# Turning probabilities and attention results by DMA crossbar transposes in place of TensorE, in an attention layer with residual and layer norm

## The chip, the cores and the metric

The kernel runs on one core of one Trainium2 chip. The metric is the device time of one execution in microseconds. The times given for a kernel are those of several runs; one further execution was recorded by the hardware profiler.

## What is computed

64 graphs of 128 nodes, each node with 512 features in 16 heads of 32. Masked attention, output projection, residual, layer norm:

```python
q = heads(x @ Wq + bq); k = heads(x @ Wk + bk); v = heads(x @ Wv + bv)
scores = jnp.einsum('bhqd,bhkd->bhqk', q, k) * scale
scores = jnp.where(mask[:, None] == 0, -jnp.inf, scores)
attn = jax.nn.softmax(scores, axis=-1)
out = jnp.einsum('bhqk,bhkd->bhqd', attn, v)
out = out.transpose(0, 2, 1, 3).reshape(b, s, D_MODEL)
x = _layernorm(x + out @ Wo + bo, axis=-1)
```

All arrays are float32.

## The kernel before

Float32 products are made from pairs of float16: a value is split into a high part (rounded to float16, by ScalarE, ACT) and a low part (the remainder, by VectorE, DVE), and TensorE (PE) multiplies hi x hi, hi x lo and lo x hi into one float32 sum.

The work runs in 32 groups of 2 batches. A group has 8 steps; step s takes the scores of 4 heads of one batch (s // 4 is the batch, s % 4 the heads). Every engine runs an order written out by hand, with semaphores between the engines; groups 2 to 29 are a loop whose body is two groups. In the same step as the attention of group g, PE also works on a projection bank: `TASKS` says which. The Q and K banks (24 matmuls of 256 columns) and V banks (12 of 512) are those of group g+1; the Y banks are the output projection of a batch finished earlier.

The path of the four heads of a step, before:

1. PE: `scores`, four matmuls of a stacked Q by a stacked K (`q_stack`, `k_stack`, where high and low parts lie under one another on the partitions) into `score_ps`.
2. DVE: `masked_max`, mask added and row minimum taken, four instructions each with an accumulator read.
3. ACT: `exponentials`, four activations into `probs`, float32.
4. PE: `transpose_probs`, four float32 transposes into `pT_ps`.
5. ACT: `high_part_probs` makes `pT_hi` from PSUM. DVE: `low_part_probs` makes `pT_lo` from PSUM.
6. PE: `attend`, eight small matmuls into `av_ps`. The attention of step s-1 is done in step s, behind the scores of step s+1.
7. DVE: `head_norm`. GpSimd (POOL): `attn_sum`, into `attn`.

When a batch's four steps are through, PE turns `attn` by four float32 transposes into `aT_ps` (`transpose_attn`); ACT and DVE split it into `aT_hi` and `aT_lo`; the Y bank multiplies by the output weights; DVE adds the residual and takes the moments (`y_and_moments`); POOL normalizes and SP stores. POOL also makes the residual (`x_res`) and the low part of the next inputs (`xT_lo`).

The Q and K stacks of group g+1 are made by DMA in SyncE's (SP's) queue. `spread_rows` takes eight DMAs of 64 KB for each of Q and K, from the split parts in `part` to the stack; `copy_rows` waits until they have landed and then doubles rows in the stack (two DMAs of 256 KB for Q, one of 512 KB for K). The scores of step 0 wait for both. SP's other DMAs load x in two layouts and the adjacency, and store the result.

## Time and profile before

| | |
|---|---|
| runs | 1017.27 us median of 3 (1017.2 to 1017.75) |
| the profiled execution's own time | 1017.49 us |
| its span in the trace | 1015.5 us |
| granted TensorE clock | 0.987 of full speed |
| busy: PE, DVE, ACT, POOL | 94%, 83%, 66%, 36% |
| instructions of PE's matmul row | 8968 |

A busy share is the part of the span in which an engine has an instruction under way. Matmuls are pipelined, so the distance between the starts of two of them says more than their durations. The trace gives for idle time of an engine what ended it, as "<-engine tile". "issue" means that no other engine's event did. SPq is SyncE's queue; its rows are the times for which issuing a DMA held the queue, and the landing of a DMA is told apart from that.

### The profile page before, as it was taken

The numbers are of one execution on the slowest core, as the hardware profiler recorded it, in microseconds if no ns is written. First come the engines' busy times: TensorE is split into PE (matmuls) and PEld (weight loads), VectorE is DVE, ScalarE is ACT, GpSimd is POOL, SyncE is SP. The second block draws the span as 40 slices with busy tenths as digits, with TensorE's granted clock in tenths as the row PEclk, the third lists the DMA queues.
The fourth block names the chain that finished last, engine by engine and source line by source line (L and its number), as shares of the span: only waits on it lengthen the run. The fifth ranks groups of instructions, "written<-read, shape, count | busy, mean of one in ns | idle before, by whom it ended". The sixth has DMA issues, their size and how long they took to land.

```text
span 1015.5 us, 29711 instructions
## 1 busy us (share of the span) xinstructions
PE 958.5 (94%) x8968; PEld 716.7 (71%) x8968; DVE 840.9 (83%) x3449; ACT 675.2 (66%) x1745; POOL 370.4 (36%) x643
## 2 busy tenths in 40 slices
PE   6799999999999999999999999999999999999974
PEld 4566776767777776777767777776777777677752
DVE  5478987888988888988888888788898888898885
ACT  5456776767767666776767767676776766677662
POOL 0043343334334333334333434333433433333332
PEclk9899999999999999999999999999999999999988
DMA  6535344454444445344445434445444444534420
GB/s 244 151 109 129 108 131 121 134 136 129 114 123 126 129 132 150 94 129 124 133 124 150 118 106 139 120 134 137 129 114 123 123 131 133 151 93 129 116 58 32
DMA packets 103790, 127.02 MB, mean 125 GB/s; under 512 B 12561, under 2 KB 82193, under 8 KB 99217
## 3 DMA queue, kind: packets, MB, share of 16 engines
q1 hardware_dynamic: 103696, 126.15, 44.1%
q14 instruction: 80, 0.65, 0.2%
q8 instruction: 14, 0.23, 0.1%
HBM read 42.21 MB, written 16.78 MB: 58 GB/s over the span
## 4 chain that ended last, share of the span: by engine, by line
PE 64%; issue 14%; DVE 12%; POOL 5%; DMA 1%; SPq 1%; POOLq 1%; DVEq 0%; ACT 0%; ACTq 0%
PE proj_ps L732 45%; PE pT_ps L830 8%; PE score_ps L732 4%; PE av_ps L732 4%; DVE masked L599 3%; PE aT_ps L744 2%; DVE pT_lo L585 2%; POOL x_res L373 2%; POOL attn L382 1%; DVE stats L630 1%; DVE kT_lo L576 1%; SPq L295 1%; POOL y L403 1%; DVE y L626 1%; DVE attn_parts L613 1%
## 5 line engine op out<-in xcount | busy, mean ns | idle before, releaser
L491 ACT ACTIVATE probs<-masked,minus_max 128x128 f32<-128x128 f32 x1024 | 325.6, 391 | 66.6 <-DVE minus_max L599 65.0
L382 POOL TENSOR_TENSOR attn<-attn_parts 128x128 f32<-128x128 f32 x256 | 116.9, 457 | 610.1 <-DVE attn_parts L613 610.1
L599 DVE CUSTOM_DVE_ANT_0 masked<-score_ps,mask 128x128 f32<-128x128 f32 x1024 | 236.0, 286 | 119.2 <-PE score_ps L732 73.6
L501 ACT ACTIVATE pT_hi<-pT_ps 128x512 f16<-128x512 f32 x256 | 152.7, 596 | 171.6 <-PE pT_ps L830 166.3
L585 DVE SCALAR_TENSOR_TENSOR pT_lo<-pT_ps,pT_hi 128x512 f16<-128x512 f32 x256 | 174.2, 681 | 0.4 <-ACT pT_hi L501 0.4
L830 PE MATMUL pT_ps<-ident,probs 128*128 128x128 f32 x1024 | 163.8, 283 | 2.6 <-ACT probs L491 0.9
L732 PE MATMUL proj_ps<-xT_hi,wq_hi 128*128 128x256 f16 x512 | 141.4, 276 | 7.9 <-DVE wq_lo L701 7.9
L732 PE MATMUL proj_ps<-xT_lo,wq_hi 128*128 128x256 f16 x512 | 141.5, 276 | 0.0
L732 PE MATMUL proj_ps<-xT_hi,wq_lo 128*128 128x256 f16 x512 | 141.5, 276 | 0.0
L732 PE MATMUL proj_ps<-xT_hi,wk_hi 128*128 128x256 f16 x512 | 139.5, 273 | 0.0
L732 PE MATMUL proj_ps<-xT_hi,wk_lo 128*128 128x256 f16 x512 | 139.5, 273 | 0.0
L732 PE MATMUL proj_ps<-xT_lo,wk_hi 128*128 128x256 f16 x512 | 139.5, 273 | 0.0
L613 DVE TENSOR_TENSOR attn_parts<-av_ps,inv_sum 128x256 f32<-128x256 f32 x256 | 108.7, 425 | 11.3
L732 PE MATMUL av_ps<-v_parts,pT_hi 128*128 128x65 f16 x1024 | 93.4, 192 | 19.5 <-DVE pT_lo L585 19.5
L732 PE MATMUL score_ps<-k_stack,q_stack 128*128 128x128 f16 x1024 | 99.7, 220 | 12.5 <-DMA k_stack<-k_stack 9.0
L830 PEld LDWEIGHTS pT_ps<-ident,probs 128*128 128x128 f32 x1024 | 108.2, 141 | 4.2 <-issue 3.0
L732 PEld LDWEIGHTS score_ps<-k_stack,q_stack 128*128 128x128 f16 x1024 | 77.6, 98 | 40.4 <-issue 18.8
L732 PE MATMUL proj_ps<-wo_hi,aT_hi 128*128 128x512 f16 x256 | 98.4, 385 | 1.4 <-DVE aT_lo L559 1.4
L732 PE MATMUL proj_ps<-wo_hi,aT_lo 128*128 128x512 f16 x256 | 98.3, 384 | 0.0
L732 PE MATMUL proj_ps<-wo_lo,aT_hi 128*128 128x512 f16 x256 | 98.2, 384 | 0.0
L732 PE MATMUL proj_ps<-wv_hi,xT_hi 128*128 128x512 f16 x256 | 97.0, 379 | 0.0
L732 PE MATMUL proj_ps<-wv_lo,xT_hi 128*128 128x512 f16 x256 | 97.0, 379 | 0.0
(62 smaller groups left out, 1832.2 us busy)
## 6 DMA issues: line engine op xcount, KB each, us to landing
xT_raw<-x_cols SPq DMA_DIRECT2D x32, 512.0 KB, 4.8
q_stack<-q_stack SPq DMA_DIRECT2D x64, 256.0 KB, 3.5
k_stack<-k_stack SPq DMA_DIRECT2D x32, 512.0 KB, 4.4
x_in<-x_rows SPq DMA_DIRECT2D x32, 512.0 KB, 3.9
out<-y SPq DMA_DIRECT2D x64, 256.0 KB, 2.2
q_stack<-qT_hi SPq DMA_DIRECT2D x128, 64.0 KB, 2.0
q_stack<-qT_lo SPq DMA_DIRECT2D x128, 64.0 KB, 2.0
k_stack<-kT_hi SPq DMA_DIRECT2D x128, 64.0 KB, 2.2
```

The lines of the kernel that those rows point to most:

```text
L295: sp.dma_start(heads[QUAD * quad:QUAD * (quad + 1), :, j, :], part[n, h][rows]).then_inc(spread[n][par], 16)
L373: pool.tensor_tensor(x_res[:, par, b], x_in[par][:, b], b_out[:], ALU.add).then_inc(res_made, 1)
L382: pool.tensor_tensor(attn[b][:, c * P:(c + 1) * P].rearrange("p (h d) -> p h d", h=HC), attn_parts[s % 2][:, :, V_LO:V_LO + DH], attn_part ...
L403: pool.tensor_scalar(y[b][:], y[b][:], minus_mean[b][:], inv_std[b][:], ALU.add, ALU.mult).then_inc(ln_done, 1)
L491: ins = act.activation(probs[s % 2][:, j], masked[s % 2][:, j], ACT.Exp, bias=minus_max[s % 2][:, j:j + 1], scale=-1.0)
L501: act.activation(pT_hi[s % 2][:], pT_ps[s % 2][:], ACT.Copy, scale=P_UP).then_inc(pT_hi_done, 1)
L585: dve.scalar_tensor_tensor(out=pT_lo[s % 2][:], in0=pT_ps[s % 2][:], scalar=P_UP, in1=pT_hi[s % 2][:], op0=ALU.mult, op1=ALU.subtract).the ...
L599: ins = dve.tensor_tensor_reduce(masked[s % 2][:, j], score_ps[s % 2][:, j], mask[par][:, s // KC], -EXP_SCALE, 3.0e38, ALU.add, ALU.min, ...
L613: dve.tensor_tensor(attn_parts[s % 2][:], av_view[:, :, 0:2 * DH], inv_sum[s % 2][:].unsqueeze(2).to_broadcast([P, HC, 2 * DH]), ALU.mult) ...
L732: return pe.matmul(dst, lhsT, rhs, start=first, stop=last)
L744: ins = pe.transpose(aT_ps[:, c], attn[b][:, c * P:(c + 1) * P], ident[:])
L830: ins = pe.transpose(pT_ps[s % 2][:, j], probs[s % 2][:, j], ident[:])
```

## The change

Probabilities are no longer turned by PE. ACT splits the high part of `probs` in row layout into the left half of a float16 tile `p_pair`, DVE puts the low part into the right half, and SP issues one DMA crossbar transpose (`dma_start_transpose`) of the 128 x 1024 tile into `pT`, from which PE's `attend` reads. `p_pair` has 2 buffers, `pT` has 4. The attention result goes the same way through `a_pair` and `aT`, one transpose a batch. Step s on PE is now: bank, scores of step s+1, attention of step s-2. The PSUM freed by the transposes gives four projection banks in place of two and two for the attention product. `TASKS` puts the Y banks in slots 4 and 7. The mask instruction becomes a scalar_tensor_tensor with a broadcast tile as second input. Loads, stores and copies have new places in SP's order.

```diff
-    TASKS = {0: (Q, 0), 1: (Q, 1), 2: (K, 0), 3: (K, 1), 4: (Y, 1), 5: (V, 0), 6: (V, 1), 7: (Y, 0), 8: (Y, 1)}
+    TASKS = ((Q, 0), (Q, 1), (K, 0), (K, 1), (Y, 0), (V, 0), (V, 1), (Y, 1))
+    NB = 4
...
-        probs = [sb(f"probs{i}", [P, HC, S], F32) for i in range(2)]
-        pT_hi = [sb(f"pT_hi{i}", [P, HC, S], F16) for i in range(2)]
-        pT_lo = [sb(f"pT_lo{i}", [P, HC, S], F16) for i in range(2)]
+        probs = [sb(f"probs{i}", [P, HW], F32) for i in range(2)]
+        p_pair = [sb(f"p_pair{i}", [P, 2 * HW], F16) for i in range(2)]
+        pT = [sb(f"pT{i}", [P, 2 * HC, S], F16) for i in range(NT)]
...
+            def turn_probs(g, s):
+                u = unit(g, s)
+                sp.wait_ge(p_lo_done, u + 1)
+                sp.sem_inc(sync_goes, 1)
+                wait(sp, av_done, u - NT + 1)
+                sp.sem_inc(sync_goes, 1)
+                sp.dma_start_transpose(pT[s % NT][:], p_pair[s % 2][:]).then_inc(p_turned[s % NT], 16)
+            def turn_attn(g, b):
+                n = batch(g, b)
+                sp.wait_ge(a_lo_done, n + 1)
...
+                sp.dma_start_transpose(aT[b][:], a_pair[b][:]).then_inc(a_turned[b], 16)
...
+                for s in range(SLOTS):
+                    before, slot = back(g, s, 1)
+                    if exists(before):
+                        turn_probs(before, slot)
...
+                    if s == 2 and at_least(g, 1):
+                        turn_attn(g - 1, 0)
...
+                    if s == 3 and has_next(g):
+                        spread_rows(Q, g + 1, nxt)
+                    if s == 4 and has_next(g):
+                        copy_rows(Q, g + 1, nxt, k + par)
+                    if s == 5 and at_least(g, 1):
+                        turn_attn(g - 1, 1)
+                    if s == 5 and has_next(g):
+                        spread_rows(K, g + 1, nxt)
+                    if s == 6 and has_next(g):
+                        copy_rows(K, g + 1, nxt, k + par)
...
+            def high_part_probs(g, s):
+                act.wait_ge(exp_done, unit(g, s) + 1)
+                before, slot = back(g, s, 2)
+                if exists(before):
+                    act.wait_ge(p_turned[slot % NT], 16 * turn_round(before, slot))
+                act.activation(p_pair[s % 2][:, 0:HW], probs[s % 2][:], ACT.Copy, scale=P_UP).then_inc(p_hi_done, 1)
...
             def low_part_probs(g, s):
-                dve.wait_ge(pT_hi_done, unit(g, s) + 1)
-                dve.scalar_tensor_tensor(out=pT_lo[s % 2][:], in0=pT_ps[s % 2][:], scalar=P_UP, in1=pT_hi[s % 2][:],
-                                         op0=ALU.mult, op1=ALU.subtract).then_inc(pT_out, 1)
+                dve.wait_ge(p_hi_done, unit(g, s) + 1)
+                dve.scalar_tensor_tensor(out=p_pair[s % 2][:, HW:2 * HW], in0=probs[s % 2][:], scalar=P_UP,
+                                         in1=p_pair[s % 2][:, 0:HW], op0=ALU.mult,
+                                         op1=ALU.subtract).then_inc(p_lo_done, 1)
...
-                dve.tensor_scalar(mask[par][:], adj_in[par][:], 0.0, MASKED, ALU.is_equal,
-                                  ALU.mult).then_inc(mask_made, 1)
+                dve.scalar_tensor_tensor(out=mask[par][:].rearrange("p b t -> p (b t)"),
+                                         in0=adj_in[par][:].rearrange("p b t -> p (b t)"), scalar=0.0,
+                                         in1=masked_out[:].to_broadcast([P, TOK]), op0=ALU.is_equal,
+                                         op1=ALU.mult).then_inc(mask_made, 1)
...
-            def transpose_probs(g, s):
-                u = unit(g, s)
-                pe.wait_ge(exp_done, u + 1)
-                wait(pe, pT_out, u - 1)
-                for j in range(HC):
-                    ins = pe.transpose(pT_ps[s % 2][:, j], probs[s % 2][:, j], ident[:])
-                ins.then_inc(pT_done, 1)
...
             def group(g, par, k):
                 nxt = 1 - par
                 for s in range(SLOTS):
...
+                    step_bank(g, s, par)
                     if s < SLOTS - 1:
                         scores(g, s + 1, par, k)
-                    else:
+                    elif has_next(g):
                         scores(g + 1, 0, nxt, k + par)
...
+                    before, slot = back(g, s, 2)
+                    if exists(before):
+                        attend(before, slot, par if s >= 2 else nxt)
```

DVE's order in a group, before and after (in `group` of the vector block; `bank_to_split` and `filled` are the slot whose bank is split there):

```python
# before
masked_max(g, s, par)
low_part_bank(g, filled, par)
head_norm(g, s - 2)
low_part_probs(g, s - 1)
# after
low_part_probs(before, slot)      # before, slot = back(g, s, 1)
masked_max(g, s, par)
low_part_bank(g + 1, *TASKS[s - 1], nxt)
head_norm(before, slot)           # before, slot = back(g, s, 3)
```

DVE's instructions in the first group of the loop, in steps 1 and 2. Each masked head is a pair of rows (the instruction and its accumulator read). Before:

```order
L599 ISA masked1,minus_max1<-score_ps1,mask0 128x128
L599 ISA minus_max1 128x1
L608 RECIPROCAL inv_sum1<-av_ps 128x4
L118 REGISTER_ALU
L613 TENSOR_TENSOR attn_parts1<-av_ps,inv_sum1 128x256
L566 ISA
L576 SCALAR_TENSOR_TENSOR qT_lo<-proj_ps1,b_qk_up,qT_hi 128x256 x2
L585 SCALAR_TENSOR_TENSOR pT_lo0<-pT_ps0,pT_hi0 128x512
L591 REGISTER_ALU
L599 ISA masked0,minus_max0<-score_ps0,mask0 128x128
L599 ISA minus_max0 128x1
```

After, from the split of the Q bank in step 1 to the first masked head of step 2:

```order
L526 SCALAR_TENSOR_TENSOR qT_lo<-proj_ps0,b_qk_up,qT_hi 128x256 x2
L553 REGISTER_ALU
L554 RECIPROCAL inv_sum0<-av_ps0 128x4
L84 REGISTER_ALU
L558 TENSOR_TENSOR attn_parts0<-av_ps0,inv_sum0 128x256
L511 ISA
L512 SCALAR_TENSOR_TENSOR a_pair0<-attn0,a_pair0 128x512
L533 SCALAR_TENSOR_TENSOR p_pair1<-probs1,p_pair1 128x512
L539 REGISTER_ALU
L546 ISA masked0,minus_max0<-score_ps0,mask0 128x128
L546 ISA minus_max0 128x1
```

Before, the low part at the end of step 1 is that of step 0 (buffer 0), ahead of the masked scores of step 2 (buffer 0). After, the low part ahead of the masked scores of step 2 is that of step 1 (buffer 1), the step whose scores were masked last.

SP's issues in the same group, from the Q copies on. ISA and REGISTER_ALU rows are waits and their registers. Before:

```order
L306 DMA q_stack1<-q_stack1 32x4096
L307 DMA q_stack1<-q_stack1 32x4096
L289 REGISTER_ALU
L295 DMA k_stack1<-kT_hi 32x4x256
L295 DMA k_stack1<-kT_lo 32x4x256
```

After, from the end of the Q spreads to the start of the K spreads:

```order
L256 DMA q_stack1<-qT_lo 32x1024
L270 REGISTER_ALU
L275 DMA_TRANSPOSE pT3<-p_pair1 128x8x128
L261 ISA
L265 DMA q_stack1<-q_stack1 32x4096
L266 DMA q_stack1<-q_stack1 32x4096
L270 REGISTER_ALU
L275 DMA_TRANSPOSE pT0<-p_pair0 128x8x128
L279 REGISTER_ALU
L284 DMA_TRANSPOSE aT1<-a_pair1 128x8x128
L252 REGISTER_ALU
L256 DMA k_stack1<-kT_hi 32x1024
```

One transpose now stands between the Q spreads and the Q copies, and two between the Q copies and the K spreads.

## Rows read from the trace of the kernel before

**Rows 1.** The page: its first line, and the busy line.

```profile
span 1015.5 us, 29711 instructions
PE 958.5 (94%) x8968; PEld 716.7 (71%) x8968; DVE 840.9 (83%) x3449; ACT 675.2 (66%) x1745; POOL 370.4 (36%) x643
```

**Rows 2.** Table by stages, 100 to 900 us: busy of each engine (instructions), clock, DMA share, GB/s.

```profile
100.00:900.00 800.00, 781.72 (x7443) 590.95 (x7442) 685.63 (x2836) 550.89 (x1432) 308.58 (x530) 1.00 0.45 127
```

**Rows 3.** Timeline of DVE: the mask in group 15 and in group 30.

```profile
510.51 1.28 DVE L646 TENSOR_SCALAR mask<-adj_in 128x256 f32<-128x256 int32 x1
...
961.86 0.28 DVE L646 TENSOR_SCALAR mask<-adj_in 128x256 f32<-128x256 int32 x1
```

**Rows 4.** Waits of DVE: us in total, times, longest.

```profile
DVE masked L599 <- issue: 37.8, 14, 4.2
```

**Rows 5.** Timeline of PE: scores, transposes, next bank, next scores (start, us).

```profile
503.57 0.39 PE L732 MATMUL score_ps<-k_stack,q_stack 128*128 128x128 f16 x4
...
504.02 0.63 PE L830 MATMUL pT_ps<-ident,probs 128*128 128x128 f32 x4
504.49 0.27 PE L732 MATMUL proj_ps<-xT_hi,wk_hi 128*128 128x256 f16 x1
...
507.11 0.39 PE L732 MATMUL score_ps<-k_stack,q_stack 128*128 128x128 f16 x4
```

**Rows 6.** Timeline of DVE, a step with y and its moments.

```profile
511.71 0.28 DVE L599 CUSTOM_DVE_ANT_0 masked<-score_ps,mask 128x128 f32<-128x128 f32 x1
...
512.55 0.08 DVE L599 DVE_READ_ACCUMULATOR2_ANT minus_max<- 128x1 f32 x1
...
513.10 0.68 DVE L585 SCALAR_TENSOR_TENSOR pT_lo<-pT_ps,pT_hi 128x512 f16<-128x512 f32 x1
513.70 0.68 DVE L626 SCALAR_TENSOR_TENSOR y<-proj_ps,x_res 128x512 f32<-128x512 f32 x1
...
515.59 0.29 DVE L599 CUSTOM_DVE_ANT_0 masked<-score_ps,mask 128x128 f32<-128x128 f32 x1
```

**Rows 7.** Timeline of ACT, one row; groups by line, two rows (busy, mean ns).

```profile
512.67 1.28 ACT L491 ACTIVATE probs<-masked,minus_max 128x128 f32<-128x128 f32 x4 [0.33 <-DVE minus_max L599]
...
L701 DVE SCALAR_TENSOR_TENSOR wo_lo<-w_land,wo_hi 128x512 f16<-128x512 f32 x4 | 2.5, 684 | 0.0
...
L534 ACT ACTIVATE wo_hi<-w_land 128x512 f16<-128x512 f32 x4 | 2.2, 618 | 0.0
```

**Rows 8.** Timeline of SP's queue: Q copy, last two K spreads, K copy, store.

```profile
508.96 0.56 SPq L306 DMA_DIRECT2D q_stack<-q_stack  x1
...
514.42 0.60 SPq L295 DMA_DIRECT2D k_stack<-kT_hi  x1
515.06 0.60 SPq L295 DMA_DIRECT2D k_stack<-kT_lo  x1
517.08 0.51 SPq L304 DMA_DIRECT2D k_stack<-k_stack  x1
520.51 0.36 SPq L312 DMA_DIRECT2D out<-y  x1
```

**Rows 9.** DMA issues: times, KB each, median us to landing.

```profile
q_stack<-q_stack SPq DMA_DIRECT2D x64, 256.0 KB, 3.5
k_stack<-k_stack SPq DMA_DIRECT2D x32, 512.0 KB, 4.4
```

**Rows 10.** Timeline of POOL in group 15.

```profile
506.53 0.46 POOL L382 TENSOR_TENSOR attn<-attn_parts 128x128 f32<-128x128 f32 x1 [1.96 <-DVE attn_parts L613]
506.95 1.27 POOL L373 TENSOR_TENSOR x_res<-x_in,b_out 128x512 f32<-128x512 f32 x1
...
510.49 1.16 POOL L259 TENSOR_TENSOR xT_lo<-xT_raw,xT_hi 128x512 f16<-128x512 f32 x1
```

**Rows 11.** The masked scores' line: duration min/median/max, first and last start.

```profile
L599 DVE CUSTOM_DVE_ANT_0 masked<-score_ps,mask x1024: 275/286/293, 37.2 to 994.5; 128x128 f32<-128x128 f32 x171
```

**Rows 12.** DMA from 503.5 to 508 us: packets, MB, share of 16 engines.

```profile
q1 hardware_dynamic: 1008, 0.46, 39.6%
```

More of the change, by code:

```diff
@@ L118, in wait, with at_least @@
             eng.wait_ge(sem, value)
+    def at_least(g, n):
+        return not isinstance(g, int) or g >= n
     def has_next(g):
@@ L124, in has_x_next2, with back, exists, all_groups @@
         return not isinstance(g, int) or g < LAST - 1
-    def all_groups(eng, group, first=None, last=None):
-        (first or group)(0, 0, 0)
+    def back(g, s, lag):
+        return (g, s - lag) if s >= lag else (g - 1, s - lag + SLOTS)
+    def exists(g):
+        return not isinstance(g, int) or g >= 0
+    def all_groups(eng, group):
+        group(0, 0, 0)
         group(1, 1, 0)
@@ L134, in all_groups @@
         group(NG - 2, 0, NG // 2 - 1)
-        (last or group)(NG - 1, 1, NG // 2 - 1)
+        group(NG - 1, 1, NG // 2 - 1)
     with ExitStack() as ctx:
@@ L211, in build_program @@
         stored = [sem(f"stored{i}") for i in range(2)]
+        p_turned = [sem(f"p_turned{i}") for i in range(NT)]
+        a_turned = [sem(f"a_turned{i}") for i in range(2)]
         const_made = sem("const_made")
@@ L358, in _ @@
             all_groups(sp, group)
-            store(LAST, 0)
-            store(LAST, 1)
+            turn_probs(LAST, SLOTS - 1)
+            turn_attn(LAST, 0)
+            store(LAST - 1, 1)
+            turn_attn(LAST, 1)
+            for b in range(GB):
+                store(LAST, b)
             for b in range(GB):
@@ L429, in _ @@
-            pool.memset(ident[:], 0.0).then_inc(const_made, 1)
-            pool.wait_ge(const_made, 1)
-            pool.affine_select(out=ident[:], in_=ident[:], compare_op=ALU.not_equal, fill=1.0, base=0,
-                               pattern=[[-1, P]], channel_multiplier=1).then_inc(const_made, 1)
+                    before, slot = back(g, s, 3)
+                    if exists(before):
+                        attn_sum(before, slot)
+                    if s == 1 and at_least(g, 2):
+                        normalize(g - 2, 1)
@@ L632, in y_and_moments @@
                 dve.wait_ge(stats_done, n + 1)
[L633 removed]
+                if at_least(g, 1):
                     dve.wait_ge(ln_done, batch(g - 1, b) + 1)
@@ new lines, in group @@
+                    before, slot = back(g, s, 1)
+                    if exists(before):
+                        low_part_probs(before, slot)
+                    masked_max(g, s, par)
+                    if s > 0 and TASKS[s - 1][0] != Y and has_next(g):
+                        low_part_bank(g + 1, *TASKS[s - 1], nxt)
+                    before, slot = back(g, s, 3)
+                    if exists(before):
+                        head_norm(before, slot)
+                    if s == 0 and at_least(g, 2):
+                        y_and_moments(g - 2, 1, par)
@@ L685, in group @@
+                    if s == 1 and at_least(g, 1):
+                        low_part_attn(g - 1, 0)
+                    if s == 4 and at_least(g, 1):
+                        low_part_attn(g - 1, 1)
+                    if s == 5 and at_least(g, 1):
+                        y_and_moments(g - 1, 0, nxt)
+                    if s == 1 and not at_least(g, 1):
                         dve.wait_ge(b_out_mm, 1)
@@ new lines, in y_bank @@
+            def y_bank(g, b):
+                pe.wait_ge(a_turned[b], 16 * (g + 1))
+                dst = proj_ps[bank_of(Y, b)]
+                for ki in range(KC):
+                    if not at_least(g, 1):
+                        weight_made("o", ki)
+                    mm(dst[:], aT[b][:, ki], w_hi["o"][:, ki], ki == 0, False)
+                    mm(dst[:], aT[b][:, ki], w_lo["o"][:, ki], False, False)
+                    ins = mm(dst[:], aT[b][:, KC + ki], w_hi["o"][:, ki], False, ki == KC - 1)
+                ins.then_inc(y_mm, 1)
@@ new lines, in _ @@
+            pe.wait_ge(w_loaded["o"][0], 16)
+            pe.wait_ge(bias_made, 2)
+            for ki in range(KC):
+                ins = mm(b_out_ps[:], b_v_wide[:, ki], w_raw["o"][:, ki], ki == 0, ki == KC - 1)
+            ins.then_inc(b_out_mm, 1)
+            scores(0, 0, 0, 0)
+            all_groups(pe, group)
+            attend(LAST, SLOTS - 2, LAST % 2)
+            pe.wait_ge(y_summed, batch(LAST - 1, 0) + 1)
+            y_bank(LAST, 0)
+            attend(LAST, SLOTS - 1, LAST % 2)
```

529 lines of the change are left out of this document (206 added, 323 removed).

## The prediction

> **What bounds the kernel now.** I read the page first: TensorE (PE) is busy 94% of the span, VectorE (DVE) 83% [rows 1]. The table over 100 to 900 us says that this is no average over unlike stages: PE 782 of 800 us, at full clock, DVE 686, DMA engines 45% [rows 2]. The mask is made once a group; two of them stand 451.4 us and 15 groups apart [rows 3], so a group (2 batches, 8 steps) takes 30.1 us, against 31 of them in the span. In the list of waits DVE stands idle 14 times 2.7 us, once per turn of the loop, under "issue" [rows 4]. TensorE's instruction stream is the bound; every other engine fits around it.
>
> **What the change takes from TensorE.** The four probability transposes of a step hold PE from 504.02 to 504.49, 0.47 us [rows 5]. Ten such sets a group (8 for probabilities, 2 for the attention result) are 4.7 us, and PE needs 25.4 us a group. If PE stayed the bound, 32 groups would save 150 us: 867 us. So the question is what the next bound is.
>
> **The loop between DVE and ScalarE (ACT).** Before, the high and low parts of the probabilities were split after the transpose, and DVE wrote them last in its step. Now both split in row layout, and DVE's order has the low part of step s-1 *ahead* of the masked scores of step s. With that, one closed loop runs through both engines: low part(s-1), masked(s), exp(s), high part(s), low part(s). Its pieces: low part 0.60 from start to next start, masked 0.92 from the first head's start to the end of the fourth head's accumulator read [rows 6], hand-over 0.04, exp 1.28 [rows 7], then the high part. That reads SBUF now instead of PSUM; the same form on the same engine is wo_hi<-w_land, 0.62 us, and DVE's low part from SBUF is wo_lo<-w_land, 0.68 [rows 7], what it took from PSUM, so the new source saves nothing. With two more hand-overs: 0.60 + 0.92 + 0.04 + 1.28 + 0.05 + 0.62 + 0.05 = 3.56 us a step. PE's step would be 3.07 (3.54 from scores to scores, less 0.47). Two steps of a group carry y_and_moments, which the gap in the loop doesn't hold: from the last masked head to the low part 0.55, y and its moments 1.89, low part 0.60, masked 0.84 [rows 6], 3.9 in all, 0.3 too much. Loop alone: 8 x 3.56 + 0.6 = 29.1 us a group. Of 30.1 this gives back 1.0 us, not 4.7.
>
> **The DMA queue of SyncE (SP).** SP issues in program order, and each issue holds it: a spread DMA 0.60 (0.64 from one to the next), eight of them 5.2, copies 0.5 to 0.6, a store 0.36 [rows 8]. A group costs SP 16 x 0.64 + 3.7 = 13.9 us now, plus waits for landings. Ten transposes come on top, woven between spreads and copies. Call t what one transpose holds the queue for. No transpose by DMA stands in the trace. Lower bound 0.36 (the shortest issue); upper bound 2.9, eight blocks of 128x128 at that price each; I take 0.64, the spread's, the nearest row that moves rows between SBUF partitions with a broken pattern. Landing: at least 3.5 us, the 256 KB copy's [rows 9].
>
> Which wait ends last in a group? The scores of the next group need the K stack. I follow SP from the masked scores of step 3, which start 3 x 3.56 + 0.3 = 11.0 us into the group. The low part of step 2 is just done (0.1); its transpose t; eight Q spreads 5.2; the Q copies wait for the last spread to land, 1.4 beyond its issue (515.06 to 517.08 for K [rows 8], less 0.6), in which the next transpose fits; two copies 1.2; then the step 4 transpose and one of the attention result, 2t; eight K spreads 5.2; landing 1.4, again with a transpose under it; the K copy lands after 4.4 [rows 9]; scores 0.4 [rows 5]. Sum 19.3 + 3t. The period is therefore 11.0 + 19.3 + 3t = 30.3 + 3t, 32.2 us with t = 0.64. The loop needs 29.1 and waits 3 us per group for the K stack. That wait also covers DVE's loop-turn gap of 2.7 us, which costs nothing more; without that cover it would be 1.35 a group. Before, SP reached the K spreads right behind the Q copies, and PE's slower step gave them time.
>
> **DVE against GpSimd (POOL).** The mask took 0.28 us when POOL was idle and 1.28 beside POOL's 1.16 us xT_lo, ending 0.14 after it [rows 3, 10]: DVE was kept out. The low part of the probabilities, which read PSUM and one SBUF tile, now reads two SBUF tiles; the mask no longer has its old form. If it meets the same exclusion, then in step 2 POOL's sum (0.46) and x_res (1.27) start 2.4 us after the masked scores and end at 4.1, where the low part could start at 2.96: 1.1 us later. Steps 4, 6 and 7 have a residual or xT_lo too (3.2 us more), but there the K stack is waited for anyway. Bounds: 0, or 1.1 plus 0.5 for the meeting in step 1. I take 1.1: 33.3 us a group.
> The Trainium skill, "SBUF — State Buffer", section "Who interferes with whom", speaks for the collision: a DVE instruction with two SBUF inputs contends with a GpSimd instruction that reads SBUF, and with at most one, outside the fast modes, it doesn't. By this rule 33.3 stands, and without it the sum is 32.2 a group, 1090 us. The trace shows the lock only on the mask.
>
> **The sum.** First masked scores at 37.2 us [rows 11] as before; first group 32.0 (no y terms, no collision); 30 groups x 33.3 = 999; seven steps of the last group 25.5 (there PE had no projections, and before ran steps of 2 to 3.6 us; the loop doesn't get shorter); from the last masked scores to the end 21 us before [rows 1, 11], and two more round trips of a DMA transpose at 3.5 each in place of PE transposes, less what PE took, about 27. That is 1121 span, and with the 2.0 us between span and execution (1017.49 against 1015.5; the median of the runs is 1017.27) 1123 us. What a measurement can't tell from no change is 0.2%, 2 us.
>
> **Rivals.**
> *The queue is held longer (t near 1.6).* For: a transpose has 128 rows x 8 blocks, 1024 pieces, a spread 128. Against: the copy of 8 KB rows and the spread of 512 B rows hold SP alike, so pieces don't seem to be priced. Period 30.3 + 4.8 + 1.1 = 36.2, time about 1210. From t = 2 on SP itself is the bound (13.9 + 10t + 2.8 us), and t = 2.9 would give 46 us a group, about 1510.
 No row here shows it.
> *The DMA engines.* In 503.5 to 508 the spreads moved 0.46 MB in 1008 packets at 39.6% of 16 engines [rows 12], 1.78 us in all: 1.0 us for 256 KB by bytes, 1.8 for 1024 packets. Ten of them and today's 13.5 (45% of 30.1) make 24 to 32 of 33.3 us: full, not over. Beyond 2.0 us a transpose they bind; landings later than 5.7 us after the low part (3.56 - 0.1 + 0.92 + 0.04 + 1.28 + 0.05) already hold the high part two steps on, since p_pair has two buffers. At 2.5 us: 38.5 a group, about 1285; mild lateness 1160.
> *Faster.* The K stack arrives within the loop, and the loop alone rules: 37 + 31 + 30 x 29.1 + 52 + 2 = 995 us. It decides once the period is under 29.7. For: PE has 4.7 us to spare, and its projections can run ahead through four banks. Against: even t = 0 leaves 30.3, so spreads or landings would have to be shorter than their rows.
> *TensorE stays the bound* (867): only if the loop didn't exist; the order on DVE excludes it.
>
> **Chances.** Forecast as built, 1080 to 1160: 0.50. Longer hold: 0.20. DMA engines or late landings, 1160 to 1290: 0.15. Faster: 0.08. Within 0.2%: 0.03. The rest (0.04) is below 1080 but slower, or far above. The range 1055 to 1250 leaves out faster, same, and the worst of both upper cases, 0.19. Faster 0.08, same 0.03, slower 0.89.
>
> **What will show it.** PE well under 85% busy; masked scores 3.6 us apart inside a group and about 3 us extra ahead of a group's first, with PE's scores waiting for k_stack's DMA; DVE's low part waiting for ACT's high part in most steps; low parts longer than 0.68 where x_res or xT_lo runs; SP's issues near 24 us a group. Wrong if: transpose issues take much more than 0.64 (then the K stack is later by three times that), the low part shows waits for the DMA's release of p_pair (DMA engines), or steps repeat in under 3.4 us.

## The result and the profile after

The changed kernel takes 1322.22 us (median of 4 runs, 1314.91 to 1323.66), the kernel before 1017.39 in the same comparison (4 runs): ratio 1.298, interval 1.293 to 1.303. I had forecast 1123 us and a range that ended at 1250. The direction was right, the size was not: 305 us are lost, and I had seen 106 of them coming.

The page of the changed kernel, against [rows 1]:

```profile
span 1321.6 us, 28124 instructions
PE 925.9 (70%) x7688; PEld 620.5 (47%) x7688; DVE 860.4 (65%) x3449; ACT 693.3 (52%) x1745; POOL 431.9 (33%) x642
...
q1 hardware_dynamic: 392464, 210.07, 72.9%
...
SPq 38%; issue 14%; PE 14%; DMA 14%; DVE 12%; ACT 7%; DVEq 1%; POOL 0%; ACTq 0%; POOLq 0%
SPq L256 22%; DMA k_stack<-k_stack 11%; PE proj_ps L657 11%; SPq L275 11%; DVE masked L546 5%; ACT probs L460 5%; SPq L284 3%; ACT p_pair L470 3%; PE score_ps L657 2%; DVE kT_lo L526 2%; SPq L266 1%; SPq L265 1%; DVE p_pair L533 1%; DVE qT_lo L526 1%; DVE a_pair L512 1%
```

No engine is full any more. The last two rows are the chain that ended last: 38% of the span lies in SyncE's queue, most of it on the spreads (L256), then on the transposes (L275, L284), and 11% on the landing of the K copy.

The same table and stretch as [rows 2]:

```profile
100.00:900.00 800.00, 576.62 (x4834) 387.65 (x4832) 532.73 (x2164) 430.94 (x1092) 280.31 (x408) 0.87 0.75 162
```

The mask, once a group as in [rows 3], from 200 to 900 us (duration min/median/max in ns, first and last start):

```profile
L584 DVE SCALAR_TENSOR_TENSOR mask<-adj_in,masked_out x18: 414/415/416, 228.0 to 897.1; 128x256 f32<-128x256 int32 x18
```

A group takes (897.1 - 228.0) / 17 = 39.4 us where it took 30.15: 9.2 us more, in 31 groups 285 of the 305 us. All comparisons below go by this period.

The waits (us in all, times, longest):

```profile
DVE p_pair L533 <- ACT p_pair L470: 268.4, 165, 5.0
...
PE score_ps L657 <- DMA k_stack<-k_stack: 202.0, 29, 7.2
ACT p_pair L470 <- DMA pT<-p_pair: 177.9, 92, 4.5
```

TensorE waits 7 us for the K stack in nearly every group.

SyncE's queue in group 12 (counted from 0), from the transpose of step 2 on. Masked scores of the group start at 513.13, those of step 3 at 525.42:

```profile
525.72 1.24 SPq L275 DMA_TRANSPOSE pT<-p_pair  x1
527.10 0.56 SPq L256 DMA_DIRECT2D q_stack<-qT_hi  x1
...
531.50 0.59 SPq L256 DMA_DIRECT2D q_stack<-qT_lo  x1
532.36 1.26 SPq L275 DMA_TRANSPOSE pT<-p_pair  x1
533.79 0.52 SPq L265 DMA_DIRECT2D q_stack<-q_stack  x1
534.35 0.59 SPq L266 DMA_DIRECT2D q_stack<-q_stack  x1
535.22 2.49 SPq L275 DMA_TRANSPOSE pT<-p_pair  x1
537.96 1.23 SPq L284 DMA_TRANSPOSE aT<-a_pair  x1
539.31 0.52 SPq L256 DMA_DIRECT2D k_stack<-kT_hi  x1
...
543.70 0.58 SPq L256 DMA_DIRECT2D k_stack<-kT_lo  x1
544.53 1.25 SPq L275 DMA_TRANSPOSE pT<-p_pair  x1
545.84 0.58 SPq L263 DMA_DIRECT2D k_stack<-k_stack  x1
546.67 2.84 SPq L275 DMA_TRANSPOSE pT<-p_pair  x1
```

A spread holds the queue 0.59 us (0.60 before, [rows 8]); a transpose holds it 1.25, and 2.5 to 2.9 right behind a copy. The landings, against [rows 9]:

```profile
q_stack<-q_stack SPq DMA_DIRECT2D x64, 256.0 KB, 3.6
k_stack<-k_stack SPq DMA_DIRECT2D x32, 512.0 KB, 5.2
...
pT<-p_pair SPq DMA_TRANSPOSE x256, 3.1
```

What TensorE does when the K stack is there (timeline of PE; start, us):

```profile
551.19 0.60 PE L657 MATMUL score_ps<-k_stack,q_stack 128*128 128x128 f16 x4 [7.16 <-DMA k_stack<-k_stack]
...
552.13 0.42 PE L657 MATMUL proj_ps<-xT_lo,wq_hi 128*128 128x256 f16 x1
552.34 0.42 PE L657 MATMUL proj_ps<-xT_hi,wq_lo 128*128 128x256 f16 x1
552.56 0.42 PE L657 MATMUL proj_ps<-xT_hi,wq_hi 128*128 128x256 f16 x1
...
556.11 0.27 PE L657 MATMUL proj_ps<-xT_hi,wq_lo 128*128 128x256 f16 x1
556.22 0.27 PE L657 MATMUL proj_ps<-xT_hi,wq_hi 128*128 128x256 f16 x1
```

Behind a wait of 7 us its matmuls of 256 columns stand 0.21 us apart, the 1.2 GHz level; near the end of the same bank, from 556.11 on, they stand 0.11 apart, 2.4 GHz. From the start of the first scores to the masked scores (552.16) it takes 0.97 us. At the higher level the kernel before needed 0.61, from the scores at 507.11 [rows 5] to this row of DVE:

```profile
507.72 0.29 DVE L599 CUSTOM_DVE_ANT_0 masked<-score_ps,mask 128x128 f32<-128x128 f32 x1 [0.67 <-PE score_ps L732]
```

The prediction had allowed 0.4, the matmuls alone. So 0.36 us of the difference is the lower clock and 0.2 the hand-over.

Last, the low part beside GpSimd in step 2, against [rows 6, 10]. DVE's timeline:

```profile
523.94 1.55 DVE L533 SCALAR_TENSOR_TENSOR p_pair<-probs,p_pair 128x512 f16<-128x512 f32 x1 [0.76 <-ACT p_pair L470]
```

POOL's timeline at the same place:

```profile
523.68 1.27 POOL L359 TENSOR_TENSOR x_res<-x_in,b_out 128x512 f32<-128x512 f32 x1
```

The low part needed 0.68 from PSUM; here it ends 0.54 us after x_res does.

### The profile page after: what moved, and what is told of

Read it like the earlier page. It is cut to its first block, busy times and chain, and to the rows that moved or that the text cites. A ratio compares the mean times of both kernels' runs of the same rounds, so it can differ in the third digit from the quotient of the medians.

```text
span 1321.6 us, 28124 instructions
## 1 busy us (share of the span) xinstructions
PE 925.9 (70%) x7688; PEld 620.5 (47%) x7688; DVE 860.4 (65%) x3449; ACT 693.3 (52%) x1745; POOL 431.9 (33%) x642
## 3 DMA queue, kind: packets, MB, share of 16 engines
q1 hardware_dynamic: 392464, 210.07, 72.9%
## 4 chain that ended last, share of the span: by engine, by line
SPq 38%; issue 14%; PE 14%; DMA 14%; DVE 12%; ACT 7%; DVEq 1%; POOL 0%; ACTq 0%; POOLq 0%
SPq L256 22%; DMA k_stack<-k_stack 11%; PE proj_ps L657 11%; SPq L275 11%; DVE masked L546 5%; ACT probs L460 5%; SPq L284 3%; ACT p_pair L470 3%; PE score_ps L657 2%; DVE kT_lo L526 2%; SPq L266 1%; SPq L265 1%; DVE p_pair L533 1%; DVE qT_lo L526 1%; DVE a_pair L512 1%
## 5 line engine op out<-in xcount | busy, mean ns | idle before, releaser
L533 DVE SCALAR_TENSOR_TENSOR p_pair<-probs,p_pair 128x512 f16<-128x512 f32 x256 | 212.8, 831 | 271.7 <-ACT p_pair L470 268.4
L470 ACT ACTIVATE p_pair<-probs 128x512 f16<-128x512 f32 x256 | 161.3, 630 | 187.3 <-DMA pT<-p_pair 177.9
L657 PE MATMUL proj_ps<-wo_hi,aT 128*128 128x512 f16 x512 | 167.7, 390 | 35.4 <-DMA aT<-a_pair 34.5
L657 PE MATMUL av_ps<-v_parts,pT 128*128 128x65 f16 (+1 forms) x2048 | 103.9, 192 | 116.6 <-DMA pT<-p_pair 116.5
L657 PE MATMUL proj_ps<-xT_hi,wq_hi 128*128 128x256 f16 x512 | 167.2, 327 | 8.0 <-DVE wq_lo L626 7.9
L657 PE MATMUL proj_ps<-xT_lo,wq_hi 128*128 128x256 f16 x512 | 167.0, 326 | 0.0
L657 PEld LDWEIGHTS av_ps<-v_parts,pT 128*128 128x128 f16 x2048 | 88.1, 102 | 125.4 <-DMA pT<-p_pair 124.7
L657 PE MATMUL proj_ps<-wv_hi,xT_lo 128*128 128x512 f16 x256 | 114.0, 445 | 0.0
L359 POOL TENSOR_TENSOR x_res<-x_in,b_out 128x512 f32<-128x512 f32 x64 | 94.4, 1475 | 43.1 <-DVE b_out L612 43.1
L657 PE MATMUL proj_ps<-wo_lo,aT 128*128 128x512 f16 x256 | 99.7, 390 | 0.0
```

Source lines behind the costliest of these rows:

```text
L359: pool.tensor_tensor(x_res[:, par, b], x_in[par][:, b], b_out[:], ALU.add).then_inc(res_made, 1)
L470: act.activation(p_pair[s % 2][:, 0:HW], probs[s % 2][:], ACT.Copy, scale=P_UP).then_inc(p_hi_done, 1)
L533: dve.scalar_tensor_tensor(out=p_pair[s % 2][:, HW:2 * HW], in0=probs[s % 2][:], scalar=P_UP, in1=p_pair[s % 2][:, 0:HW], op0=ALU.mult, op ...
L657: return pe.matmul(dst, lhsT, rhs, start=first, stop=last)
```

## Experiments

All start from the changed kernel unless another is named. The period is (last - first start of the mask)/(count - 1) between 200 and 900 us. The time of an experiment is the median of two runs, which lie 0.2 to 6 us apart; the four of the changed kernel lie between 1315 and 1324 us, so a difference of less than 10 us from it is none that can be told.

| kernel | us | period, us | clock | DMA share of the span |
|---|---|---|---|---|
| before | 1017 | 30.15 (209.0 to 872.4, x23) | 0.99 | 0.44 |
| changed | 1322 | 39.4 | 0.86 | 0.73 |
| x1_no_turn | 1146 | 34.1 (201.8 to 883.7, x21) | 0.89 | 0.41 |
| x2_half_spreads | 1161 | 34.1 (207.3 to 889.3, x21) | 0.90 | 0.77 |
| x3_half_turn | 1264 | 37.6 (221.0 to 898.0, x19) | 0.86 | 0.54 |
| x4_extra_load | 1342 | 40.1 (227.3 to 868.6, x17) | 0.85 | 0.72 + 0.07 |
| x5_scores_first | 1315 | 39.2 (226.6 to 893.3, x18) | 0.85 | 0.73 |
| x6_masked_first | 1342 | 40.3 (227.6 to 871.9, x17) | 0.85 | 0.72 |
| x7_k_from_pool | 1300 | 38.6 (224.7 to 881.5, x18) | 0.86 | 0.65 + 0.15 |
| x8_no_turn_both | 1139 | 34.1 (232.9 to 881.1, x20) | 0.89 | 0.41 |
| x9_interleaved | 1258 | 37.5 (219.3 to 893.7, x19) | 0.86 | 0.75 |
| x10_no_turn_interleaved | 1051 | 31.1 (221.8 to 875.7, x22) | 0.92 | 0.44 |
| x11_four_pairs | 1321 | 39.4 (225.0 to 895.2, x18) | 0.85 | 0.72 |
| x12_attn_only | 1145 | 34.2 (226.7 to 876.4, x20) | 0.94 | 0.49 |
| x13_no_copies | 1144 | 33.3 (210.1 to 875.3, x21) | 0.90 | 0.69 |
| x14_idle_pool | 1300 | 38.8 (224.6 to 883.4, x18) | 0.84 | 0.74 |
| x15_best_order | 1257 | 37.5 (215.1 to 890.1, x19) | 0.86 | 0.75 |

**What the transposes cost, and in which currency.** x1 leaves all transposes out:

```diff
-sp.dma_start_transpose(pT[s % NT][:], p_pair[s % 2][:]).then_inc(p_turned[s % NT], 16)
+sp.sem_inc(p_turned[s % NT], 16)      # and the same for aT
```

> The changed kernel with all 320 crossbar transposes left out: SP raises their semaphores at the same places in its order, and PE reads tiles filled once with a constant, so the output is not the reference's. Queue theory (the order on SP makes the K stack late; each transpose holds SP 1.25 us, some 2.5 to 2.9): the group falls from 38.9 us to 30.3 us plus up to 1.1 for the meetings with POOL, the time to 1030 to 1070 us. Engine theory (the load on the 16 DMA engines sets the time): also about 1050. Loop theory (the closed loop between DVE and ACT, with POOL's collisions, is what costs): stays above 1150 us. So this run tells the transposes from the new order of work.

1146 us, ratio 1.127 (1.123 to 1.132). Missed by 76 us: transposes make 5.3 us of the 9.2 us a group; 3.9 us stay without a single one. The loop theory's bound of 1150 is only 4 us away, so the time alone doesn't tell. The traces do: in both kernels a group is the chain from its first masked scores over SyncE's queue and the K copy to the next first masked scores. Its four pieces, as medians over groups 4 to 27 of each trace (issue and landing times; the prediction's column is its own sum, with t = 0.64 and the 1.1 us for GpSimd):

| us | prediction | changed | x1 | x3 | x5 | x6 | x14 |
|---|---|---|---|---|---|---|---|
| first masked scores to first Q spread | 12.8 | 14.8 | 13.7 | 14.0 | 14.5 | 15.6 | 13.8 |
| first Q spread to K copy | 15.7 | 18.6 | 14.6 | 17.9 | 18.6 | 18.6 | 18.6 |
| K copy's landing | 4.4 | 5.2 | 4.7 | 4.6 | 5.1 | 5.2 | 5.2 |
| landing to next masked scores | 0.4 | 1.1 | 1.1 | 1.1 | 1.1 | 1.1 | 1.1 |

Without transposes the chain loses 1.1 us ahead of the Q spreads, 4.0 between them and the K copy and 0.5 in the landing, and it is still what a group waits for.

x2 leaves out the eight low spreads of a group from the third group on (`if h == "lo" and at_least(g, 2): continue`):

> The changed kernel with the low-part spreads of Q and K left out from group 2 on (8 of 16 spread DMAs a group; the low rows of the stacks keep old values, so the output is not the reference's). Queue theory: 8 issues of 0.63 us leave SP's path to the K stack, the group falls by 5 us to 34 us, the time to about 1165 us. Engine theory: the spreads left out are 2 us of some 28 us of DMA work a group, 7%: about 1230 us.

1161 us, as the queue theory said. Eight holds of 0.63 are 5.0 us, and the period fell by 5.3.

x3 turns only the high halves (128 x 512 in place of 128 x 1024):

> The changed kernel with transposes of the high halves only (128 x 512 instead of 128 x 1024; the low halves of pT and aT keep a constant, so the output is not the reference's). It measures what the hold of SP depends on: 0.65 us if it goes by blocks, 1.25 if it is a price per instruction. Queue theory with a hold by blocks: three holds on the path shorter by 0.6 each and the long holds behind the copies shorter, 4 us a group less: about 1190 us; with a fixed hold above 1270. Engine theory: 7 of 28 us of DMA work gone, 25%: down to the loop's floor, about 1050 us.

1264 us. The issues of the probability transposes (duration ns min/median/max), here and in the changed kernel:

```profile
L276 SPq DMA_TRANSPOSE pT<-p_pair x256: 1189/1210/2522, 41.1 to 1236.3; - x128
```

```profile
L275 SPq DMA_TRANSPOSE pT<-p_pair x256: 1232/1253/2970, 40.3 to 1294.2; - x128
```

Half the data holds the queue 1.21 instead of 1.25 us where no copy is under way: nearly a fixed price an instruction. Right behind the Q copies the hold falls from 2.4 to 1.8 us and behind the K copy from 2.9 to 2.4, so the long holds do depend on the data. By the table above the 1.8 us a group that came back are 0.8 ahead of the Q spreads, 0.7 between them and the K copy and 0.6 in the K copy's landing (4.6 instead of 5.2; a transpose lands in 2.4 instead of 3.1). The theory of full DMA engines, 1050 us, fell.

x4 adds four copies of 256 KB a group, issued by ScalarE:

> The changed kernel with one more 256 KB copy between two spare tiles in every second step, issued by ACT (4 a group, none on SP). Engine theory: DMA work goes from 28 to 31.5 us a group, the time up by up to 12%, about 1450 us. Queue theory: SP's order is untouched, only landings get a little later: 1325 to 1365 us.

1342 us: more load on the 16 engines costs 20 us, not 130. They are busy, but in this order of the queue they are not what sets the period.

**The order of work.** x5 and x6 change an order on TensorE and on VectorE:

```diff
 # x5, TensorE, step 0 only              # x6, VectorE, every step
-step_bank(g, 0, par)                    -low_part_probs(g, s - 1)
 scores(g, 1, par, k)                     masked_max(g, s, par)
+step_bank(g, 0, par)                    +low_part_probs(g, s - 1)
```

> In step 0 of every group TensorE does the scores of step 1 ahead of the Q bank. In the trace of the changed kernel the masked scores of steps 0 and 1 stand 5.1 us apart where other steps repeat in 3.5 to 3.6, with a Q bank at a low granted clock between them. Restart theory: the 1.5 us are given back in each of 31 groups, since SyncE's queue starts its next chain from these steps: 1322 - 46, about 1275 us. Rival, queue full by itself: SyncE's queue is busy or waiting for landings all through the group, the steps that are done earlier wait longer at its end: 1310 to 1325 us.

> VectorE takes the masked scores of step s ahead of the low part of step s-1, so the closed loop low part - masked - exp - high part - low part is broken. Loop theory (the steps' length is the main loss): steps fall from 3.6 to 4.1 us to about 3.1, seven times a group, some 4 us a group, about 1200 us. Queue theory: the masked steps come 0.4 us closer, but each transpose is handed to SyncE's queue 0.9 us later, and the group's period is still set by what the queue issues before the K stack: 1290 to 1330 us.

1315 and 1342 us: 7 less, which is within the changed kernel's own spread, and 20 more, 12 above the queue theory's range. Neither edit shortened the stretch that counts, from the first masked scores to the Q spreads. In x5 step 0 fell from 5.0 to 3.75 us and step 1 grew from 3.7 to 4.55 by the bank that now stands there, so the spreads start only 0.3 us earlier. In x6 steps 1 to 4 did get shorter (2.8 to 3.7 us, where they were 3.5 to 4.5), but the low part of step 2 ends later behind the masked scores of step 3: the Q spreads start 0.7 us later, and the period grew by 0.9. So x6 shows that shorter steps in themselves give nothing back; it doesn't show that the steps ahead of the Q spreads are free, and x14 below shows that they aren't.

> All transposes are left out (as in the first run of this study, 1146 us; the attention multiplies by constant tiles), and besides the two edits of order above are made: masked scores ahead of the low part, and scores of step 1 ahead of the Q bank. It shows what the new order of work costs without any transpose. Order theory: 1.5 us for the restart and about 0.4 x 7 us for the loop come back per group, 31 x 4.3 = 133 us: about 1015 us. Rival, stacks still bound: the K stack's chain of spreads, landing and copy in SyncE's queue stays the limit even without transposes: 1090 to 1146 us, with TensorE still waiting 4 us or more a group for the K stack.

x8, both edits without transposes, gives 1139 and the period of x1, 34.1: still 7 us of waiting for the K stack, as the rival had it. The same cause: Q spreads stand behind step 2's low part in the queue, which starts 12 us into the group in either order, and the first spread 13.7 us in.

x9 leaves everything as it is but SyncE's order: spreads in fours, a step earlier, K copy ahead of a transpose (the edit in outline, conditions left out):

```diff
-if s == 3: spread_rows(Q, g + 1, nxt)
-if s == 5: turn_attn(g - 1, 1); spread_rows(K, g + 1, nxt)
-if s == 6: copy_rows(K, ...)
+if s in (2, 3): spread_rows(Q, g + 1, nxt, half=s - 2)
+if s in (4, 5): spread_rows(K, g + 1, nxt, half=s - 4)
+if s == 5: turn_attn(g - 1, 1)
+if s == 6: copy_rows(K, ...)            # ahead of turn_probs
```

> SyncE's order alone is changed: the Q spreads are issued in two fours at the ends of steps 2 and 3 (before: eight in step 3), the K spreads in two fours in steps 4 and 5, the K copy at the start of step 6, ahead of that step's transpose. Chain theory: the period of a group is the time from its first masked scores to the start of the Q spreads plus the chain spreads, landing, copies, spreads, landing, copy; it falls because the chain starts a step earlier and the K copy no longer stands behind a transpose. K copy at about 24 us into the group, landing 5.2, scores 1: about 32 us a group where 39.4 were, 1322 - 31 x 7 = about 1100 us, at most 1200. Engine theory: the 16 DMA engines were 73% busy over 39.4 us, 28.7 us a group, and more per us makes each landing longer: no less than 36 us a group, 1220 us or more.

1258 us: better by 64, far from the 1100 I expected, and in the engine theory's range. TensorE waits for the K stack only once in the whole run; it waits for transposes, 169 us for the probabilities and 137 us for the attention result, whose transpose now stands behind the K spreads (timeline of PE):

```profile
515.10 0.52 PE L658 MATMUL av_ps<-v_parts,pT 128*128 128x65 f16 x8 [2.71 <-DMA pT<-p_pair]
519.42 0.59 PE L658 MATMUL proj_ps<-wo_hi,aT 128*128 128x512 f16 x1 [3.80 <-DMA aT<-a_pair]
```

> All transposes left out, masked scores ahead of the low part, scores of step 1 ahead of the Q bank (1139 us in an earlier run), and now the stacks interleaved as in the run beside this one. Chain theory: without transposes the 34.1 us of a group were still the stacks' chain, and a chain started a step earlier takes 5 us or more off: 28 to 30 us a group, 960 to 1010 us, TensorE's wait for the K stack under 2 us a group. Rival, collisions and restarts: if low parts held up by GpSimd and the low granted clock make the period, the new order of DMAs changes little: 1100 to 1139 us.

The same order without transposes (and with x5 and x6) gives 1051 us, between the two theories: 31.1 us a group, 3.0 us less than x8. So those 3 us of the 3.9 that x1 left over were the place of the stacks' chain in the queue. With transposes in it (37.5) the same order is 6.4 us a group longer, though the edits of x5 and x6 are in that difference too. x10 still isn't free of the queue's order: TensorE waits 31 times, 79 us in all, for SyncE to release the attention result, which stands behind the K spreads although nothing is transposed.

x11 gives p_pair four buffers; x15 is x9, x11 and x5 together:

> p_pair gets four buffers in place of two, so that ScalarE's high part no longer waits for the landing of the transpose of two steps before (178 us of waits in the changed kernel). Chain theory: these waits fall in steps 5 to 7, behind the start of the stacks' chain, and are covered by the wait for the K stack: 1305 to 1325 us. Late-landing theory (steps held by p_pair set the time): up to 178 us less, about 1200 us.

> The interleaved order of SyncE's queue (1258 us in an earlier run), four p_pair buffers, and scores of step 1 ahead of the Q bank, nothing left out. In the interleaved run TensorE no longer waited for the K stack; ScalarE waited 137.6 us of 700 for landings of transposes (p_pair), TensorE 77 us for aT. Latency theory: what holds the interleaved kernel are landings that reach into the loop through two buffers; with four, 7 us a group come free and the steps or TensorE's wait for aT rule: 33 to 34.5 us a group, 1120 to 1170 us. Engine theory: 28.7 us of DMA engine time a group cannot be packed much closer than 37.5 us: 1240 to 1260 us. Neither expects less than the kernel before.

1321 us for x11, the changed kernel's time, and 1257 for x15, that of x9: the buffers bring nothing in either. The 178 us that ScalarE waited for p_pair were covered. x15 lies in the engine theory's range too. Its TensorE waits for the landings as long as that of x9 (100.6 and 77.4 us there); the waits of 200 to 900 us in x15:

```profile
PE av_ps L658 <- DMA pT<-p_pair: 101.3, 57, 2.8
PE proj_ps L658 <- DMA aT<-a_pair: 77.6, 37, 3.9
```

**The queue or the engines behind it.** x7 has GpSimd issue the K spreads and the K copy.

> The eight K spreads and the K copy of a group are issued by GpSimd instead of SyncE, the data moved stays the same. Queue theory: SyncE loses 8 x 0.63 + 0.5 us of holds and the K stack no longer stands behind transposes; the wait of TensorE for the K stack, 7 us a group, falls to 2 us or less as long as GpSimd issues one in about 1 us: 1130 to 1200 us. DMA engine theory (the 16 engines are full): same bytes and packets, so no more than 20 us change: 1300 to 1340 us. If GpSimd takes far longer than 1 us for an issue, attn_sum and x_res come late behind it and the time stays above 1250 though SyncE is free; then the waits for attn and x_res show it.

1300 us, at the edge of the engine theory's range and 100 above the queue theory's. TensorE's wait for the K stack did fall, from 202 to 46 us, but its wait for the transposed probabilities rose from 117 to 206. GpSimd issues one in 0.5 us, but look at the landings:

```profile
k_stack<-k_stack POOLq DMA_DIRECT2D x32, 512.0 KB, 4.7
...
k_stack<-kT_hi POOLq DMA_DIRECT2D x128, 64.0 KB, 5.6
```

A K spread that landed in 2.0 us now takes 5.6, beside SyncE's copies and transposes, and two transposes issued one after the other meanwhile hold SyncE's queue 5.5 us. Two queues do not add up here: what one gains the other waits.

x13 leaves the Q and K copies out from the third group on:

> From the third group on the Q and K copies are left out (the stacks' doubled rows keep old values), the spreads, all transposes and the waits for the spreads' landing stay. The trace of the changed kernel has transposes that hold the queue 1.25 us, and those right behind a copy 2.5 to 2.9. Backlog theory (a transpose is held while a large transfer issued just ahead is under way): no transpose above 1.4 us any more; the period loses the landing of the K copy and the scores behind it (5.8), two issues of copies (1.15) and one long hold (1.24), and then the loop of the steps rules at about 32 us: about 1095 us. Rival, the long hold belongs to the place (two transposes one after the other, the landing of the spreads): holds of 2.5 us stay, period 33 us or more, 1125 us or more.

1144 us. The long holds are gone (timeline of SP's queue):

```profile
531.47 2.95 SPq L277 DMA_TRANSPOSE pT<-p_pair  x2
534.68 1.23 SPq L286 DMA_TRANSPOSE aT<-a_pair  x1
...
541.37 2.82 SPq L277 DMA_TRANSPOSE pT<-p_pair  x2
```

A row of x2 is two transposes with the time between them: here 1.27 and 1.24, then 1.25 and 1.23 us. The second of the first pair stands where the Q copies were and held 2.49 in the changed kernel, the second of the last pair where the K copy was and held 2.84. In x9 two transposes come behind the K copy:

```profile
517.47 0.59 SPq L264 DMA_DIRECT2D k_stack<-k_stack  x1
518.33 4.54 SPq L276 DMA_TRANSPOSE pT<-p_pair  x2
```

The first of them holds 2.84 us and the second 1.45. So a transpose issued behind a large copy under way is held longer, as the backlog theory says, but not until the copy has landed: this copy lands at 522.7, and the first transpose is through at 521.2. In the changed kernel the long holds end 1.1 us (Q) and 1.5 us (K) ahead of the last copy's landing, in the median of 20 groups each. The time came out 50 us above the theory's sum and in the rival's range (33.3 us a group for 32). TensorE's wait for pT's landing grew from 117 to 153 us in all.

x14 leaves out GpSimd's x_res and xT_lo from the third group on:

> From the third group on GpSimd leaves out x_res and xT_lo (the sum and the low part keep old values), all waits stay. Exclusion theory, as in the prediction (1.1 us a group for the meeting in step 2, the others covered by the wait for the K stack): steps 2 to 3 go from 4.49 us to 3.6, the low part's mean from 831 ns to under 710, and the time falls by 31 x 0.94 = 29 us to about 1293. Rival 1, covered everywhere: 1315 to 1325. Rival 2, all meetings count (steps 2, 6 and 7): 31 x 2.2 = 68 us less, 1254.

1300 us: 22 less, 0.6 us a group where 0.94 was expected. Steps 2 to 3 went from 4.50 to 3.63 us and the low part's mean from 831 to 728 ns. The exclusion is real, and in step 2 it is on the path: the Q spreads start 1.0 us earlier in a group. This fits the exclusion theory, with the meetings of the other steps covered.

**One part alone.** x12 is the kernel before with only the attention result split in row layout and turned by DMA, two transposes a group (the edit in outline):

```diff
 # SyncE, group g                                  # PE, steps 1 and 5
+turn_attn(g - 1, 1)  # amid the Q spreads         -transpose_attn(...)
+turn_attn(g, 0)      # ahead of the K copy
```

> The kernel before, with one part of the change alone: the attention result is split in row layout and turned by a DMA transpose (two a group), probabilities stay with TensorE. One transpose stands in the middle of the Q spreads, one ahead of the K copy. TensorE loses 2 x 0.47 us of 30.1 a group. If TensorE stays the bound: 1017 - 29 = 988 us. Chain theory: before, the K stack landed just in time (it was waited for 9 us in all), each transpose ahead of it holds the queue 1.25 us, so the K stack comes up to 2.5 us later in each group: 1030 to 1065 us.

1145 us, ratio 1.125 (1.121 to 1.130): neither theory. The K stack stays in time (6.8 us of waits in all); it is the Y bank that waits (timeline of PE):

```profile
512.77 0.61 PE L749 MATMUL proj_ps<-wo_hi,aT 128*128 128x512 f16 x1 [3.58 <-DMA aT<-a_pair]
```

DVE ends the low part at 508.87, the queue is free since 507.0, and SyncE issues the transpose at 509.11; it lands at 512.65. TensorE would have gone on at 509.2. So here it isn't the place in the queue but the 3.5 us from issue to landing that a transpose on TensorE doesn't have. Behind that wait the first eight of the bank's twelve matmuls start 0.43 us apart, the last ones 0.21: the 1.2 GHz level again. Two transposes a group cost 4.0 us of the period and save TensorE 0.94. The order of the banks is that of the kernel before; a later place for the Y bank, as in the changed kernel, wasn't tried with this part alone.

## Why the prediction was wrong

**Right:** TensorE falls out of the critical chain (70% busy, "well under 85%"); SyncE's in-order queue makes the K stack late, and TensorE waits for it; low part against x_res in step 2. The spreads' price of 0.64, their landing of 1.4 and the places of the transposes in the queue held too. Of its other signs, the wait ahead of a group's first scores is 7 us and not 3, and SP's issues hold the queue 28.6 us a group and not 24. Row by row for the group above, from the masked scores of step 3 (525.42) to those of the next step 0 (552.16):

| piece of the prediction's chain | predicted, us | measured, us |
|---|---|---|
| hand-over and transpose of step 2 | 0.1 + t = 0.74 | 1.68 |
| Q spreads, landing | 5.2 + 1.4 | 5.26 + 1.43 |
| Q copies | 1.2 | 1.43 |
| transpose of step 4, transpose of aT | 2t = 1.28 | 4.09 |
| K spreads, landing | 5.2 + 1.4 | 5.22 + 1.31 |
| K copy to first scores | 4.4 | 5.35 |
| scores to masked scores | 0.4 | 0.97 |
| sum | 21.2 | 26.7 |
| masked scores of step 0 to step 3 | 11.0 + 1.1 | 12.3 |

**The step that failed is "I take 0.64, the spread's"**, the term t. Its three places cost 5.77 us where 2.02 were allowed: 3.75 us of the 5.7 missed in this group. The holds themselves are 1.24, 2.49 and 1.23 us, 4.96 where 3t = 1.92 was put; the other 0.8 are the hand-over and the 0.1 to 0.3 us between issues, for which the sum had 0.1. The nearest row was of the wrong kind, and that a transpose behind a copy could be held longer than elsewhere wasn't considered. The rival with t = 1.6 had nearly the right size, the mean of the three being 1.65, and I gave it 0.20. Its argument for a longer hold, priced by pieces, was wrong for the plain hold all the same: x3 halves the pieces and 1.25 becomes 1.21. Its 36.2 us a group is still 3.2 short of the 39.4. The Trainium skill ("DMA: Bandwidth & Descriptors", table of sequencer cycles) led in the prediction to an estimate of 1.7 us; this chip shows 1.25, less than that, and the page has nothing on the 2.5 to 2.9 behind a copy.

**What the sum left out.** From the K copy's issue to the first scores it takes 5.35 us instead of 4.4. About 0.5 of that come with the transposes (landing 5.2, in x1 4.7); why x1 still has 0.3 more than the kernel before isn't shown. The row of 0.4 for the scores left out the hand-over to DVE, 0.2 us, which the kernel before shows. And the wait itself costs: behind 7 us of idle time the first scores and a large part of the Q bank run at the 1.2 GHz level, 0.36 us on the chain and up to 1.7 in the step from 0 to 1 (4.0 to 5.6 us, median 5.0, where 3.56 + 0.3 was reckoned). The group of the table above had one of the short ones, 4.06, so the table shows less of this than most groups have. In the loop of the kernel before the granted clock is 1.00 [rows 2], so none of the rows that the prediction used could show it. Over the span, 30 groups x 6.1 us are 182 of the 199 us missed; the rest lies in the first and last groups.

**Where the loss of 305 us went**, as far as runs show: about 5.3 us of the 9.2 a group come with the transposes (x1), most of it as time in the queue; about 3 with the new place of the stacks' chain, which starts only behind step 2's low part (x8 against x10, both without transposes); the exclusion makes 0.6 (x14). The three were measured in different kernels and needn't add up. Of the closed loop, on which the prediction spent most of its second part, the steps up to the low part of step 2 are on the path, 12.3 us of the group in the table, and were put nearly right at 12.1; the later steps are covered by the wait for the K stack. Of the exclusion the rule of the Trainium skill ("SBUF — State Buffer", "Who interferes with whom") held: a low part with two SBUF inputs took 1.55 us beside x_res and 0.69 without; 1.1 was reckoned for it and 0.87 found in the step.

**What stays open.** In x9 and x15 the period is 37.5 us though nothing in it is full (TensorE 75%, DMA engines 77% of 200 to 900 us). The trace shows waits for aT and pT in turn. Both times lie where the engine theory had put them, and no run with more or less DMA load was made from x9, so for this order the load on the engines stays a rival. Whether a third order of the queue would spread the waits better wasn't tried. Nor was it measured what x10 would take without its wait for the release of the attention result, 2.6 us in nearly every group. No version beat the kernel before.

## What to carry to other kernels

Work moved from a full engine to a DMA queue is paid in that queue's order: price the hold of each issue and follow the transfer that the next stage waits for, not the mean share of the DMA engines. An operation that the trace doesn't have carries its uncertainty as often as it stands in one serial chain; here three times, and once at twice the price because a large copy was under way ahead of it. Data turned by DMA came 3 us after the issue, more than 5 behind a copy. The consumer must be able to wait that long; in x12's order two transposes a group were already too many.

## What the runs showed of the hardware

- A DMA transpose of 128 x 1024 float16 from SBUF to SBUF held SyncE's queue 1.25 us and landed in 3.1; 128 x 512 held it 1.21 and landed in 2.4.
- Per transpose the queue moved (392464 - 54544) / 320 = 1056 packets of some 250 bytes, and took (0.729 x 1321.6 - 0.405 x 1144.8) / 320 = 1.56 us of all 16 engines for 256 KB.
- A transpose behind copies under way was held longer: 2.5 us behind 2 x 256 KB, 2.8 to 2.9 behind 512 KB, and let go 1.1 to 1.5 us before the last copy had landed. Without the copies it was held 1.25 (x13). Plain DMAs behind copies were mostly held 0.4 to 0.9; but in x12 the load of x, issued behind a transpose, the K copy and a store, was held 2.0 us in each of 23 groups (0.36 in the kernel before).
- GpSimd issued a 64 KB DMA in 0.5 us, less than SyncE's 0.59.
- Behind 7 us of idle time TensorE's matmul starts stood 0.21 us apart from 512.9 to 515.0 in group 12 (2.9 us after the first scores) and from 552.1 to 556.0 in group 13 (4.8 us after them), then 0.11. The stretch at the lower level isn't the same from group to group.
